# Second attention: the expert scores' matmuls and the next tile's transposes at other places of TensorE's order

## The reference

```python
shift = silu(t) @ W_ada.T + b_ada
h = ln(x, ln1_g, ln1_b) + shift
qkv = (h @ Wqkv.T).reshape(b, n, 3, 16, 64)
q, k = ln(qkv[:, :, 0], qn_g, qn_b), ln(qkv[:, :, 1], kn_g, kn_b)
scores = einsum('bhnd,bhmd->bhnm', q, k) / sqrt(64)
o = einsum('bhnm,bhmd->bhnd', softmax(scores), v)
x = x + o @ Wout.T
gate = softmax(x.reshape(-1, 256) @ Wgate.T)      # expert scores, 8 experts
# each expert takes its 1024 best tokens, runs an MLP on them, and adds its weighted result
```

## Time and profile before

| | us |
|---|---|
| median of 3 runs | 2479.66 (2479.55 to 2481.01) |
| the profiled execution's own time | 2483.42 |
| its span | 2481.6 |
| TensorE busy | 2349.0 (95%) |
| TensorE's weight loads busy | 2077.4 (84%) |
| VectorE busy | 1906.0 (77%) |
| ScalarE busy | 1552.9 (63%) |
| GpSimd busy | 1038.9 (42%) |
| second attention, the steady part | about 900 to 1920 us of the span |

### The profile page before, as it was taken

The page is one execution under the profiler, slowest core; times in us unless marked ns, Lnnn a source line. Parts: engine busy times, 40 slices in busy tenths (PEclk is TensorE's granted clock), DMA queues, the critical chain, the costliest instruction groups (busy, mean ns, idle before and its releaser), DMA issues. The chain is left out here.

```text
span 2481.6 us, 67114 instructions
## 1 busy us (share of the span) xinstructions
PE 2349.0 (95%) x24912; PEld 2077.4 (84%) x24912; DVE 1906.0 (77%) x3763; ACT 1552.9 (63%) x2982; POOL 1038.9 (42%) x939
## 2 busy tenths in 40 slices
PE   7999999999999899999999999999999727999997
PEld 5888888799999788888888888888888626999996
DVE  6999999776666688888888888888888686666663
ACT  5888888766666465656556565655656454556553
POOL 4888888400000143434434344343434203445543
PEclk8999999999999899999999999999999856999998
DMA  4111110110110100000000000000000122333423
GB/s 142 39 38 42 38 39 27 49 33 21 32 32 21 37 14 16 15 17 13 17 13 17 17 13 17 13 17 13 17 17 13 36 38 70 91 92 84 96 50 34
DMA packets 78720, 89.21 MB, mean 36 GB/s; under 512 B 18480, under 2 KB 72496, under 8 KB 76080
## 3 DMA queue, kind: packets, MB, share of 16 engines
q1 hardware_dynamic: 66352, 71.10, 9.2%
q0 software_dynamic: 12288, 17.05, 4.2%
HBM read 62.42 MB, written 25.69 MB: 36 GB/s over the span
## 5 line engine op out<-in xcount | busy, mean ns | idle before, releaser
L1275 POOL TENSOR_TENSOR a_rq<-a_vq,minus_half 128x8 f32<-128x8 f32 x256 | 417.6, 1641 | 97.9 <-DVE a_vq L1299 97.9
L1222 ACT ACTIVATE a_sq<-a_bqk 128x512 f32<-128x512 f32 x256 | 152.8, 597 | 351.3 <-PE a_bqk L126 351.3
L1270 POOL TENSOR_TENSOR a_rstd<-a_veps,minus_half 128x1 f32<-128x1 f32 x63 | 34.8, 552 | 580.4 <-DVE a_veps L1346 580.4
L124 PE MATMUL a_bqk<-wqk_hi,a_h_lo 128*128 128x512 f32 x512 | 207.6, 405 | 3.5 <-DVE a_h_lo L1315 3.5
L126 PE MATMUL a_bqk<-wqk_hi,a_h_hi 128*128 128x512 f32 x512 | 201.2, 393 | 0.0
L125 PE MATMUL a_bqk<-wqk_lo,a_h_hi 128*128 128x512 f32 x512 | 201.0, 393 | 0.0
L1291 DVE TENSOR_TENSOR a_qk<-a_bqk,a_rq 128x512 f32<-128x512 f32 x256 | 175.9, 687 | 29.8 <-POOL a_rq L1275 29.7
L1899 ACT ACTIVATE e_u<-e_bu,e_b 128x512 f32<-128x512 f32 x128 | 88.3, 690 | 157.1 <-PE e_bu L126 155.2
L2041 DVE TENSOR_TENSOR e_u_lo<-e_u,e_u_hi 128x512 fp32r<-128x512 f32 x128 | 88.9, 695 | 127.1 <-ACT e_u_hi L1904 126.4
L1207 ACT COPY a_vs<-a_ba 64x512 f32<-64x512 f32 x256 | 148.8, 581 | 53.6 <-PE a_ba L126 48.9
L1283 DVE TENSOR_REDUCE a_ss<-a_sq 128x8 f32<-128x512 f32 x256 | 173.7, 679 | 2.7 <-ACT a_sq L1222 1.0
(11 more groups left out here) (329 smaller groups left out, 8057.0 us busy)
## 6 DMA issues: line engine op xcount, KB each, us to landing
a_qk<-gates_of_rows SPq DMA_DIRECT2D x32, 256.0 KB, 4.3
tokens<-a_xs SPq DMA_DIRECT2D x64, 128.0 KB, 1.7
out<-a_xs SPq DMA_DIRECT2D x64, 128.0 KB, 1.7
e_w<-in_fc1s SPq DMA_DIRECT2D x8, 1024.0 KB, 5.0
e_w<-in_fc2s SPq DMA_DIRECT2D x8, 1024.0 KB, 4.8
a_gate<-gates_of_rows SPq DMA_DIRECT2D x122, 64.0 KB, 2.5
X<-in_x SPq DMA_DIRECT2D x56, 128.0 KB, 2.1
wst<-in_qkv_w SPq DMA_DIRECT2D x16, 128.0 KB, 2.5
```

The source lines that it names most:

```text
L124: tensor.matmul(to, w_lo, x_hi, start=start, stop=False)
L1222: nc.scalar.activation(sq[:, n * BK:(n + 1) * BK], b_qk[:, n * BK:(n + 1) * BK], ACT.Square).then_inc(s["sq"], 1)
L1275: nc.gpsimd.tensor_tensor(rq[:, 8 * n:8 * n + 8], vq[:, 8 * n:8 * n + 8], g.mhalf[:, 0:8], ALU.pow).then_inc(s["rq"], 1)
```

## The change

The gate moves from behind `turn_qk(2, 4)` to ahead of P V, and waits for two copies of values of this tile where it waited for all four. `turn_qk` is cut after its first group of four transposes and no longer after its second. `turn_next` moves from `kc` 4 to `kc` 7 of the output product, and `scores` from `kc` 6 to `kc` 7, directly behind it. The programs of the other engines are the same.

```diff
@@ TensorE's step
                 if has(0):
-                    turn_qk(0, 2)
+                    turn_qk(0, 1)
+                if has(-2):
+                    pe.wait_ge(s["xsT_out"], i - 1)
+                    if has(0):
+                        pe.wait_ge(s["v_out"], 4 * i + 2)
+                    if not has(-1):
+                        pe.wait_ge(s["lg_out"], i - 2)
+                    for kc in range(DC):
+                        last = nc.tensor.matmul(b_a[:, 0:E], xsT[:, kc, :], g.wgate[:, kc, :],
+                                                start=(kc == 0), stop=(kc == DC - 1))
+                    last.then_inc(s["lg"], 1)
                 if has(-1):
                     pe.wait_ge(s["pT_out"], 2 * i)
...
                     last.then_inc(s["o"], 1)
                 if has(0):
-                    turn_qk(2, QG)
-                if has(-2):
-                    pe.wait_ge(s["xsT_out"], i - 1)
-                    if has(0):
-                        pe.wait_ge(s["v_out"], 4 * (i + 1))
-                    if not has(-1):
-                        pe.wait_ge(s["lg_out"], i - 2)
-                    for kc in range(DC):
-                        last = nc.tensor.matmul(b_a[:, 0:E], xsT[:, kc, :], g.wgate[:, kc, :],
-                                                start=(kc == 0), stop=(kc == DC - 1))
-                    last.then_inc(s["lg"], 1)
+                    turn_qk(1, QG)
                 if has(-1):
                     if not later(i - 1):
                         pe.wait_ge(s["wout_lo"], 1)
                     for kc in range(H // 2):
                         if kc % (H // 4) == 0:
                             pe.wait_ge(s["o_lo"], 2 * (i - 1) + kc // (H // 4) + 1)
-                            if kc and has(1):
-                                turn_next()
-                        if kc == 6 and has(0):
+                        if kc == 7 and has(1):
+                            turn_next()
+                        if kc == 7 and has(0):
                             scores()
```

## The result

The changed kernel takes 2513.49 us (2512.91 to 2514.13, 4 runs) against 2479.61 before: ratio 1.0136, 95% interval 1.0123 to 1.0149, 33.9 us slower. The forecast was 2521.9 with a range of 2507 to 2534. The profiled execution spans 2511.1 us.

A forecast was written before the change was run, and what follows sets the result against it. TensorE was taken to set the pace. Per tile, a 0.24 us stall at `h_lo` plus 0.44 new at `xs` made 0.68; 62 tiles gave 42.2 us, added to 2479.66 for 2521.9 us, range 2507 to 2534.

The forecast's parts named there:

- Part 1: Gate ahead of P V, three instead of two groups of `qk` transposes behind it: worth 0.
- the release: Lag from a producer's end to TensorE's held load: 0.06 us taken at `h_lo` and `xs`, uncertain by 0 to 0.12.
- Part 2: Next tile's row transposes from the product's fifth to eighth step: VectorE's chain 1.06 us later, TensorE 0.68 us a tile.
- Part 3: Scores from before the product's seventh to before its eighth step: valued at 0, bounds 0 to 0.09 us a tile gained.
- the transposes later: Next tile's transposes in the output product: start nine matmuls later, at 0.1175 us each, so 1.06 us.
- room ahead of L1414: Ahead of the transposes of `xs`: 0.48 us of the delay is absorbed before TensorE is held.
- the exposed load: At the transposes of `xs`: a held weight load is not prefetched, costing 0.10 us, uncertain by 0 to 0.22.
- the saved switch: In the output product: transposes and scores interrupt it at one place, valued at 0, at most 0.09 us a tile gained.
- Faster: Between P V and the product: removing the gate gains 0.44 us a tile, 27 us, giving 2452; chance 0.03.
- Only `h_lo` binds: Only the wait ahead of the Q/K product costs: 0.24 us a tile, 15 us, giving 2495; chance 0.04.
- No change: Same instructions, and VectorE absorbs the delay in its 1.5 us of idle: 2480; chance 0.04.
- The whole delay is passed on: A later TensorE wait, `kT` or last scaled group, binds too: full 1.06 us a tile, 66 us, 2545; chance 0.08.

The follow-up runs named there:

- experiment 10: Kernel before with the second half of the values behind P's transposes and qk's transposes cut 4 + 12: 2465.36 us against 2480.19, ratio 0.9940.
- experiment 2: Kernel before with only the next tile's transposes and the scores moved to the product's eighth step: 2512.97 us against 2479.19, ratio 1.0135.
- 4: Kernel before with the gate ahead of P V, qk's transposes cut 4 + 12, and scores at the eighth step: 2480.21 us against 2479.88.
- experiment 1: Kernel before with only the gate ahead of P V and qk's transposes cut 4 + 12: 2496.08 us against 2479.19, ratio 1.0066.
- 6: Changed kernel with the next tile's transposes at the product's sixth instead of eighth step: 2477.57 us against 2480.19 for the kernel before, ratio 0.9991.
- 5: Changed kernel with the next tile's transposes at the product's seventh instead of eighth step: 2493.37 us against 2479.19 for the kernel before, ratio 1.0057.
- 9: Changed kernel with VectorE's statistics moved to the head of its step, ahead of `hT`: 2496.12 us against 2479.88 for the kernel before, ratio 1.0064.
- 7: Changed kernel with the transposes of `xs` behind the third instead of second Q/K group: 2499.24 us against 2480.19 for the kernel before, ratio 1.0077.
- experiment 3: Kernel before with only the scores moved from the product's seventh to its eighth step: 2480.21 us against 2479.19, ratio 1.0002.

## Why the prediction was right, and where its size was off

*The bound.* TensorE sets the pace, with two hidden holes behind `PT` and `o_lo`. Right for `o_lo`, by experiment 10. For P V the 0.12 us behind `PT` was read as a held load; in experiment 10 `PT` is early and the idle time is as long, so the wait for `PT` was hardly what cost there.

*Part 1 is worth zero.* Right: 1409.91 to 1412.53 from P V's load to the product, 2.62 us, and 2.61 in the earlier trace rows; experiments 2 and 4. What was misjudged is the release at `kT`, and with it the margin. I took the release of the scores at 0.12 us, from P V; in experiment 1 the load comes 1407.72 - 1407.41 = 0.31 us behind `kT`. It stayed covered in the change, barely: there `kT` ends at 1413.75 + 1.22 = 1414.97, with 0.31 us that is 1415.28, and the scores load at 1415.34. The margin is 0.06 us by this, where the prediction had 0.31 (1403.03 to 1403.34). That part 1 cost nothing in the change owed something to luck.

```profile
1413.75 1.22 ACT L1258 ACTIVATE a_kT<-a_bqk,kn 128x1024 f32<-128x1024 f32 x1
```

*Part 2 carries the loss through VectorE's chain.* Right in place, sign and mechanism: both waits at their marks, in all tiles, the chain moved whole; undone in full by the turn at the sixth step (6), in part by the turn at the seventh (5), a shorter chain (9) and a later reader (7), and not by anything on part 1's side. At `h_lo` two errors cancelled: its delay was 0.99 us and not 1.06, its release 0.12 and not 0.06, so the load came 0.23 us later (1404.78 - 1400.46 = 4.32 us behind the product's start, now 1417.08 - 1412.53 = 4.55) where 0.24 was forecast.

*Part 3 is worth zero.* Right (experiment 3).

*What the profile after would show.* The two new waits came, at 0.2 and 0.5 us, and the period of 17.87 for 18.0. For VectorE's idle time ahead of `hT` I had written near 2.2 us or more, taking TensorE's delay off; it is 2.50, since `o_lo` ends at the same distance from the product's start and only the 1.00 us come on top.

*The sum.* 0.68 us a tile was forecast; 33.9 / 62 = 0.55 came. The four terms, forecast and measured in the tile shown: the transposes later by 1.06, measured 2.51 - 1.51 = 1.00; the chain unchanged, measured 0.02 shorter; room ahead of L1414 0.48, measured 0.49; the exposed load 0.10, measured (1420.71 - 1420.20) - (1408.09 - 1407.64) = 0.06. So 1.00 - 0.02 - 0.49 + 0.06 = 0.55. The two mis-sized terms are the first and the last. The first took one spacing of 0.1175 us from the stretch behind the old transposes; in the changed kernel nine matmuls of the product take 1.02 us (1413.90 to 1414.92 in the tile shown). In 16 of 57 tiles the transposes are 1.07 us late (2.58 - 1.51), so the forecast of 1.06 fits those; what makes the two kinds of tile was not found. The last was taken from a product's matmul and applied to a transpose. The matmul at 1420.20 starts with its load, so a held load was not pulled ahead, which is how the prediction had read the rule of the Trainium skill ("TensorE: Matmul & The Clock Gate", "Step-by-step: what each phase is for"); only what that costs was taken too high. Each is 0.04 to 0.06 us; in 62 tiles they make 8 us, together with 0.02 of the chain and 0.01 of the room. The shift lies at the lower end of the 0.55 to 0.82 us that the prediction gave, and the time just below its 2514. Those bounds were drawn from the release, the exposed load and the saved switch; the first term, which missed most, was not among them, and the bounds do not follow from the three by adding (the first two alone give 0.68 - 0.06 - 0.10 = 0.52 to 0.68 + 0.06 + 0.12 = 0.86).

*The rivals.* None came true. "Faster" needed a product queued behind the gate; it is still behind `o_lo` (1411.78 + 0.69 = 1412.47 on VectorE, the load at 1412.53), and that hole took another order to fill (experiment 10). "Only `h_lo` binds" is what is left after experiments 7 and 9, at 16 to 19 us for the 15 it gave. "No change", from the same work on the busiest engine, is refuted by a TensorE that has as many instructions as before and 33.9 us more time for them. "The whole delay is passed on" would have been 66 us; no wait of TensorE for a scaled group is in the list, and the 0.17 us ahead of the scores are there too where `kT` is long done (experiment 2).

## What to carry to other kernels

On a busy in-order engine, a piece that other engines wait for has a slack: measure it as the distance from the end of the chain that it starts to the start of the instruction that waits for the chain's result, less what the release takes. Here `xs` ended at 1407.10, the matmul of L1414 started at 1407.64 and the release took 0.05, which gives 0.49 us, and the runs found 0.45. Its load, at 1407.42, had been pulled ahead and would have given 0.32 less the release, too little. Moved later within that slack the piece is free, and beyond it the whole further delay is paid in every tile, however idle the engine in between looks in sum. A move that is free beside another can cost by itself (part 1 costs 17 us without part 3), so the parts are timed before half of a change is kept. A hole behind another engine's result is filled with work that waits for neither: that gave the 14.8 us of experiment 10.

## What the runs showed of the hardware

A weight load that waits for another engine starts at different distances behind the producer's end: 0.05 us for `xs` (1420.15 to 1420.20), 0.06 for `o_lo` (1417.74 to 1417.80), 0.12 for `h_lo` (1416.96 to 1417.08), and 0.31 for `kT` ahead of the scores' 64x64 matmuls (1407.41 to 1407.72 in experiment 1). The prediction had worked with 0.06 for `xs` and `h_lo` and 0.12 for `kT`.

Ahead of the loads of 64x64 matmuls stand 0.17 us of idle behind transposes, where nothing is waited for too (experiments 2 and 10). It is not a fixed price: in the changed kernel P V stands behind the gate, whose loads end at 1427.16 + 0.53 = 1427.69, and P V's start 0.09 us later (0.12 behind `PT`, as before).

```profile
1427.16 0.53 PEld L1478 LDWEIGHTS a_ba<-wgate,a_xsT 128*128 128x128 f32 x4
1427.78 1.05 PEld L1491 LDWEIGHTS a_bb<-a_PT,a_vs 64*64 64x64 f32 x64
```

Whether any of this idle time is a part of the 0.31 us at `kT` is not shown.
